# Attention with a fused convolution: maxima across partitions and the output turned by VectorE, the convolution added by GpSimd, high value rows 1088 bytes apart

## What is computed

```
q = Wq x + bq;  k = Wk x + bk;  v = Wv x + bv        # x: 4 images, 256 channels, 64 x 64 pixels; q, k: 32 channels
att = softmax(q^T k / sqrt(32))                       # 4096 x 4096 an image
out = gamma * (v att^T)                               # 256 channels
fused = Wf concat(out, x) + bf                        # 1x1 convolution over 512 channels
```

## Time and profile before

| | us |
|---|---|
| median of 3 runs | 2033.55 (2033.51 to 2033.58) |
| the profiled execution: its time, its span | 2033.3, 2031.4 |
| TensorE busy (share) | 2015.3 (99%) |
| VectorE busy | 1584.9 (78%) |
| ScalarE busy | 1748.9 (86%) |
| GpSimd busy | 1206.1 (59%) |
| TensorE clock granted | 1.00 throughout |
| DMA engines busy, mean | 10% |

### The profile page before, as it was taken

One profiled execution on the slowest core, in us unless ns is written; L12 is line 12 of the kernel. 1 busy time (PEld: TensorE's weight loads), 2 busy tenths in 40 slices (PEclk: granted clock), 3 DMA queues, 4 the chain that ended last, 5 costly groups with the idle time before them and its releaser, 6 DMA issues.

```text
span 2031.4 us, 45017 instructions
## 1 busy us (share of the span) xinstructions
PE 2015.3 (99%) x16232; PEld 1980.4 (97%) x16232; DVE 1584.9 (78%) x2157; ACT 1748.9 (86%) x2373; POOL 1206.1 (59%) x514
## 2 busy tenths in 40 slices
PE   9999999999999999999999999999999999999999
PEld 8999999999899999999989999999998999999999
DVE  6788888886778888888677888888867788888885
ACT  7888888887888888888788888888878888888886
POOL 0467766667056677666605666766660666677665
PEclk9999999999999999999999999999999999999999
DMA  4200000000310000000031000000003100000000
GB/s 136 84 22 22 15 15 21 21 21 12 120 70 22 22 21 15 16 21 21 11 125 65 22 21 21 21 10 21 21 11 130 38 22 21 21 21 18 13 21 17
DMA packets 54081, 69.46 MB, mean 34 GB/s; under 512 B 4048, under 2 KB 37584, under 8 KB 53968
## 3 DMA queue, kind: packets, MB, share of 16 engines
q1 hardware_dynamic: 53696, 67.91, 10.0%
q10 hardware_dynamic: 272, 0.07, 0.0%
HBM read 34.41 MB, written 33.55 MB: 33 GB/s over the span
## 4 chain that ended last, share of the span: by engine, by line
PE 92%; DVE 3%; ACT 3%; issue 2%; DMA 0%; DVEq 0%; ACTq 0%; SPq 0%
PE ps_o L388 72%; PE ps_s L380 11%; PE ps_p L242 3%; PE ps_o L242 2%; PE ps_t L284 1%; ACT queries L478 1%; ACT hi L453 1%; DVE val_lo L676 1%; PE ps_s L259 1%; PE ps_t L276 1%; PE ps_t L269 1%; DVE top L612 1%; DVE lo L599 1%; PE ps_t L242 0%; DVE raw L626 0%
## 5 line engine op out<-in xcount | busy, mean ns | idle before, releaser
L755 POOL TENSOR_TENSOR raw<-raw,top_m 128x1024 f32<-128x1024 f32 x508 | 1205.4, 2413 | 809.1 <-ACT top_m L464 809.1
L631 DVE TENSOR_TENSOR lo<-ps_p,hi 128x1024 fp32r<-128x1024 f32 x512 | 626.9, 1224 | 311.4 <-ACT ps_p L545 311.1
L612 DVE TENSOR_TENSOR top<-ps_s,top 128x512 f32<-128x512 f32 x960 | 660.0, 687 | 55.6 <-ACT raw L459 7.4
L538 ACT ACTIVATE hi<-raw 128x1024 fp32r<-128x1024 f32 x512 | 543.9, 1062 | 145.9 <-PE ps_o L388 141.4
L388 PE MATMUL ps_o<-val_hi,hi 128*128 128x258 f32 x4096 | 664.5, 284 | 4.1 <-ACT hi L538 4.1
L388 PE MATMUL ps_o<-val_lo,hi 128*128 128x256 f32 x4096 | 652.4, 281 | 0.0
L459 ACT ACTIVATE raw<-ps_s 128x512 f32<-128x512 f32 x1024 | 554.1, 595 | 54.7 <-PE ps_s L380 32.0
L388 PE MATMUL ps_o<-val_hi,lo 128*128 128x258 f32 x4096 | 599.3, 284 | 0.0
L388 PEld LDWEIGHTS ps_o<-val_hi,hi 128*128 128x128 f32 x4096 | 562.4, 189 | 5.8 <-issue 4.6
L388 PEld LDWEIGHTS ps_o<-val_lo,hi 128*128 128x128 f32 x4096 | 560.4, 189 | 0.0
L388 PEld LDWEIGHTS ps_o<-val_hi,lo 128*128 128x128 f32 x4096 | 538.7, 190 | 0.0
(11 more groups left out here) (72 smaller groups left out, 1028.3 us busy)
## 6 DMA issues: line engine op xcount, KB each, us to landing
xf<-x SPq DMA_DIRECT2D x32, 512.0 KB, 3.7
conv_d<-conv_st SPq DMA_DIRECT2D x64, 256.0 KB, 2.0
result<-conv_d SPq DMA_DIRECT2D x64, 256.0 KB, 2.6
out<-result SPq DMA_DIRECT2D x64, 256.0 KB, 2.2
raw<-wf2T SPq DMA_DIRECT2D x1, 256.0 KB, 3.9
raw<-wv SPq DMA_DIRECT2D x1, 256.0 KB, 4.3
raw<-wf1T SPq DMA_DIRECT2D x1, 256.0 KB, 4.7
raw<-wkqT ACTq DMA_DIRECT2D x1, 64.0 KB, 2.0
```

Source lines behind the costliest of these rows:

```text
L538: nc.scalar.activation(hi[:, t % 2], raw[:, slot].rearrange("p j i -> p (j i)"), ACT.Exp, scale=SCALE).then_inc(hi_done, 1)
L612: nc.vector.tensor_tensor(top[:, new], scores, top[:, new if half else old], ALU.max).then_inc(max_done, 1)
L631: nc.vector.tensor_tensor(lo[:, t % 2], ps_p[:].rearrange("p h n -> p (h n)"), hi[:, t % 2].bitcast(F32), ALU.subtract).then_inc(lo_done, 1)
L755: nc.gpsimd.tensor_tensor(raw[:, slot], raw[:, slot], top_m[:, r].unsqueeze(1).broadcast_to((P, JQ, I)), ALU.subtract).then_inc(sub_done, 1)
```

## The change

- The turns of the maxima and of the output leave TensorE. `nc.vector.transpose` turns each 32 x 32 square by itself. The maxima: VectorE turns `top_j`, reduces over 32 (leaving eight numbers in each of 128 partitions), brings the four partition groups together with four small copies and two small maxima (`top_across`), and spreads them with another turn (`spread_top`, now in quad 6). ScalarE's copy is gone.
- As the squares are turned in place, the score products read the queries in another order (`turned`), and the output lies in 32-partition groups, so each load of the convolution and each store is four DMAs of 32 partitions with runs of 64 pixels.
- The convolution is added by GpSimd, in its own quad 4, between subtractions; at an image's end in the first chunk of the next projection.
- In the last chunk of a projection the chain of the maxima and `subtract_first` stand on VectorE before the low parts of the values; GpSimd starts after `subtract_first`, and the convolution's first half goes to `ps_t`.
- `val_hi` has rows of 272 numbers (1088 bytes) where it had 258 (1032); 258 are used as before.

```diff
-        val_hi = sb("val_hi", [P, JT, CV], F32R)
+        val_hi = sb("val_hi", [P, JT, C_IN + 16], F32R)
         val_lo = sb("val_lo", [P, JT, C_IN], F32R)
         raw = sb("raw", [P, SLOTS, JQ, I], F32)
         hi = sb("hi", [P, 2, JQ * I], F32R)
         lo = sb("lo", [P, 2, JQ * I], F32R)
         xf = sb("xf", [P, 2, KT, W], F32)
         conv_st = sb("conv_st", [P, KT, W], F32)
-        result = sb("result", [P, OUTS, KT, I], F32)
+        result = sb("result", [P, OUTS, CT, IT * SQ], F32)
+        o_turn = sb("o_turn", [P, CT, IT, SQ], F32)
         o_norm = sb("o_norm", [P, IT, C_IN], F32)
         top = sb("top", [P, 2, 2, I], F32)
         top_m = sb("top_m", [P, OUTS, I], F32)
         top_j = sb("top_j", [P, I], F32)
-        top_col = sb("top_col", [P, IT], F32)
+        top_turned = sb("top_turned", [P, I], F32)
+        top_group = sb("top_group", [P, I // 32], F32)
+        top_over = sb("top_over", [P // 2, I // 32], F32)
+        top_half = sb("top_half", [P // 2, I // 32], F32)
+        top_all = sb("top_all", [P, I // 32], F32)
...
             def load_conv(b, n):
-                sp.wait_ge(stored[n % OUTS], b * (16 * USES[n % OUTS]) + 16 * (n // OUTS + 1))
-                sp.dma_start(result[:, n % OUTS], conv_v[bass.ds(b, 1), :, :, n * I:(n + 1) * I].rearrange(
-                    "b p k n -> p (b k) n")).then_inc(conv_loaded[n % OUTS], 16)
+                sp.wait_ge(stored[n % OUTS], b * (LANDED * USES[n % OUTS]) + LANDED * (n // OUTS + 1))
+                for g in range(GROUPS):
+                    sp.dma_start(result[g * SQ:(g + 1) * SQ, n % OUTS], conv_q[
+                        bass.ds(b, 1), :, :, n * I + g * RUN:n * I + (g + 1) * RUN].rearrange(
+                        "b q c n -> q (b c) n")).then_inc(conv_loaded[n % OUTS], 16)
             def store(b, n):
                 sp.wait_ge(finished, b * BLOCKS + (n + 1))
-                sp.dma_start(out_v[bass.ds(b, 1), :, :, n * I:(n + 1) * I].rearrange("b p k n -> p (b k) n"),
-                             result[:, n % OUTS]).then_inc(stored[n % OUTS], 16)
+                for g in range(GROUPS):
+                    sp.dma_start(out_v[bass.ds(b, 1), :, :, n * I + g * RUN:n * I + (g + 1) * RUN].rearrange(
+                        "b q c n -> q (b c) n"), result[g * SQ:(g + 1) * SQ, n % OUTS]).then_inc(stored[n % OUTS], 16)
...
+            def turned(queries_of):
+                return queries_of.rearrange("r (g i q) -> r i g q", g=GROUPS, i=IT)
...
-                        last = nc.tensor.matmul(ps_s[:, (bank + half) % BANKS, jl], keys[:, j * P:(j + 1) * P],
-                                                queries[:, bass.ds(n * I, I)], start=True, stop=True)
+                        last = nc.tensor.matmul(ps_s[:, (bank + half) % BANKS, jl].rearrange(
+                            "p (i g q) -> p i g q", i=IT, g=GROUPS), keys[:, j * P:(j + 1) * P],
+                            turned(queries[:, bass.ds(n * I, I)]), start=True, stop=True)
...
-            def turn_top(B, done):
-                if done is not None:
-                    pe.wait_ge(finished, done)
-                pe.wait_ge(top_j_done, B + 1)
-                for i in range(IT):
-                    last = nc.tensor.transpose(ps_t[:, i * P:(i + 1) * P], top_j[:, i * P:(i + 1) * P], ident[:])
-                last.then_inc(top_t_ready, 1)
-            def spread_top(B):
-                pe.wait_ge(top_col_done, B + 1)
-                for i in range(IT):
-                    last = nc.tensor.transpose(ps_t[:, I + i * P:I + (i + 1) * P], top_col[:, i:i + 1].broadcast_to((P, P)), ident[:])
-                last.then_inc(m_ready, 1)
-            def turn_out(B):
-                pe.wait_ge(o_scaled, B * IT)
-                for i in range(IT):
-                    for k in range(KT):
-                        last = nc.tensor.transpose(ps_t[:, k * I + i * P:k * I + (i + 1) * P],
-                                                   o_norm[:, i, k * P:(k + 1) * P], ident[:])
-                last.then_inc(o_turned, 1)
...
-                    turn_top(b * BLOCKS, None)
-                    pe.wait_ge(q_out, C + 1)
-                    convolve(ps_p[:, 0], 0, lambda: spread_top(b * BLOCKS))
+                    pe.wait_ge(conv_done, C * 2 - 1)
+                    convolve(ps_t[:], 0)
+                    pe.wait_ge(max_done, b * HALVES + 2 * len(MADE))
                     convolve(ps_s[:, LAST_CONV].rearrange("p j i -> p (j i)"), 1)
...
-                        if t == 1 and not first:
-                            pe.wait_ge(m_done, B + 1)
-                            turn_out(B)
-                        if t == 5 and not last_block:
-                            spread_top(B + 1)
                         scores_ahead(t)
                         pe.wait_ge(lo_done, Q + (t + 1))
                         trail(t, 0)
                         trail(t, 1)
-                        if t == 4 and not last_block:
-                            turn_top(B + 1, None if first else B)
...
+            def turn_top(B):
+                dve.wait_ge(top_j_done, B + 1)
+                nc.vector.transpose(top_turned[:], top_j[:]).then_inc(top_t_done, 1)
             def reduce_turned(B):
-                dve.wait_ge(top_t_ready, B + 1)
-                nc.vector.tensor_reduce(top_col[:].unsqueeze(2), ps_t[:, 0:I].rearrange("p (i j) -> p i j", i=IT), AX_X,
-                                        ALU.max).then_inc(top_col_done, 1)
+                dve.wait_ge(top_t_done, B + 1)
+                nc.vector.tensor_reduce(top_group[:].unsqueeze(2), top_turned[:].rearrange("p (u k) -> p u k", k=32), AX_X,
+                                        ALU.max).then_inc(top_group_done, 1)
+            def top_across(B):
+                dve.wait_ge(top_group_done, B + 1)
+                nc.vector.tensor_copy(top_over[:], top_group[P // 2:P]).then_inc(half_over, 1)
+                dve.wait_ge(half_over, B + 1)
+                nc.vector.tensor_tensor(top_half[:], top_group[0:P // 2], top_over[:], ALU.max).then_inc(half_done, 1)
+                dve.wait_ge(half_done, B + 1)
+                nc.vector.tensor_copy(top_over[0:32], top_half[32:64]).then_inc(quarter_over, 1)
+                dve.wait_ge(quarter_over, B + 1)
+                nc.vector.tensor_tensor(top_all[0:32], top_half[0:32], top_over[0:32], ALU.max).then_inc(quarter_done, 1)
+                dve.wait_ge(quarter_done, B + 1)
+                nc.vector.tensor_copy(top_all[32:64], top_all[0:32]).then_inc(half_filled, 1)
+                dve.wait_ge(half_filled, B + 1)
+                nc.vector.tensor_copy(top_all[64:P], top_all[0:64]).then_inc(top_all_done, 1)
+            def spread_top(B, r):
+                dve.wait_ge(top_all_done, B + 1)
+                nc.vector.transpose(top_m[:, r], top_all[:].unsqueeze(2).broadcast_to((P, I // 32, 32))).then_inc(m_done, 1)
...
-            def add_conv(B, r, loaded):
-                dve.wait_ge(o_turned, B + 1)
-                dve.wait_ge(conv_loaded[r], loaded)
-                nc.vector.tensor_tensor(result[:, r], ps_t[:].rearrange("p (k n) -> p k n", k=KT), result[:, r],
-                                        ALU.add).then_inc(finished, 1)
+            def turn_out(B):
+                dve.wait_ge(o_scaled, (B + 1) * IT)
+                nc.vector.transpose(o_turn[:], o_norm[:].rearrange("p i (c q) -> p c i q", q=SQ)).then_inc(o_turned, 1)
...
                 if last_chunk:
                     early_scores(c)
                     reduce_top(b * HALVES + 2 * MADE[c] + 2)
+                    turn_top(b * BLOCKS)
+                    reduce_turned(b * BLOCKS)
+                    top_across(b * BLOCKS)
+                    spread_top(b * BLOCKS, 0)
+                    subtract_first(b * BLOCKS)
                     values_lo(0)
-                    reduce_turned(b * BLOCKS)
                     values_lo(1)
-                    subtract_first(b * BLOCKS)
                     split_p(b * STEPS, 0)
...
                     if t == 2 and not first:
-                        before = (r + OUTS - 1) % OUTS
-                        use = (n - 1) // OUTS if isinstance(n, int) else (n - 1 - before) // OUTS
-                        add_conv(B - 1, before, b * (16 * USES[before]) + (use * 16 + 16))
+                        turn_out(B - 1)
                     if t == 4 and not last_block:
                         reduce_top(H + 2 * 2 * QUADS)
+                        turn_top(B + 1)
                     if t == 5 and not last_block:
                         reduce_turned(B + 1)
+                        top_across(B + 1)
+                    if t == 6 and not last_block:
+                        spread_top(B + 1, (r + 1) % OUTS)
...
+            def add_conv(B, r, loaded):
+                pool.wait_ge(o_turned, B + 1)
+                pool.wait_ge(conv_loaded[r], loaded)
+                nc.gpsimd.tensor_tensor(result[:, r], o_turn[:].rearrange("p c i q -> p c (i q)"), result[:, r],
```

(49 more changed lines are left out.)

19 lines of the change are left out of this document (6 added, 13 removed).

## The result

The changed kernel takes 2064.94 us (median of 4 runs, 2062.80 to 2066.61) against 2033.57 (4 runs, 2033.51 to 2033.62): ratio 1.0154, 95% interval 1.0141 to 1.0167. The profiled execution has a span of 2061.0 us, 29.6 more than before. It is slower by 31 us; 2050 was predicted, with 2008 to 2085 as range.

The account below looks back on a forecast made before the run. TensorE was taken to bound the kernel. The terms -51.6 - 1.3 - 11.5 + 77.8 + 1.8 + 1.6 = +16.8 us on the profiled execution's 2033.3 gave 2050, range 2008 to 2085.

Parts of the forecast that it names:

- The wait: In quad 0 TensorE waits 1.39 us for a fold, 56 times: +77.8 us.
- The step that decides: From quad 6's start: maxima spread at 2.75 us, ScalarE's exponential at 5.30, fold of quad 7's first half done at 9.14.
- The transposes: Eight transposes a block leave TensorE, saving 0.86 us in each of 60 blocks: -51.6 us, and -1.3 at image starts.
- The rows 1088 bytes apart: High-row value products on TensorE go from 121.0 to about 119.6 ns over 8192 products: -11.5 us.
- the sum: All terms of the forecast added: +16.8 us on the profiled execution's 2033.3.
- Queries in runs, DMAs in fours, adds on GpSimd: Score products' broken reads, up to 33 us, taken as 0; four DMAs and 1.2 us of GpSimd adds a block hidden.
- A sign of being wrong: On TensorE, score products spaced wider than 119 ns would show the forecast wrong.
- Image starts and end: At image starts +0.45 us on TensorE's path, four times, +1.8 us; at the kernel's end +1.6 us.
- Rival (b): Slower: VectorE and GpSimd exclude each other, the chain slips 0.3 to 0.6 us, 2067 to 2084; chance 0.12.
- The margin: GpSimd's batch ends 20.3 us after the maxima, VectorE's next maximum starts 20.3 us after them: nil.
- ring: GpSimd's queue and VectorE's chain behind it, each holding the other from block to block; a 28.1 us block was predicted.
- Rival (a): Faster: TensorE's stall in quad 0 is below 1.09 us, time below 2031; chance 0.20.

Follow-up runs that it names:

- the output's part: Kernel before with only the output turned by VectorE, convolution added by GpSimd, four DMAs, rows 1088 bytes apart; maxima as before, spread in quad 5: 2009.85 us.
- two experiments: High value rows 1032 bytes apart in the changed kernel: 2065.30 us against 2064.94; 1088 in the kernel before: 2033.88 against 2033.85.
- The kernel with one small operation: Changed kernel with one 128x8 copy for the six small operations, leaving out the comparison between the four partition groups: 2009.13 us.
- the maxima's part: Kernel before with only the maxima turned, compared and spread by VectorE, spreading in quad 6; output, add, DMAs and rows as before: 2089.98 us.
- another order in quad 7: Changed kernel where, in quad 7, ScalarE copies scores before its exponentials and VectorE folds their first half before the split: 2073.34 us.

## Why the prediction was right, and where it was not

- **The wait.** The step that decides, the chain from the spreading to the fold, held. In the block with S6 = 1687.11 the maxima come at S6+2.78 (2.75 was predicted), ScalarE starts the exponential at S6+5.30 (5.30), the fold is done at S6+9.13 (9.14), and TensorE's half was due at S6+7.91 (7.88). TensorE started 0.06 us after the fold and not 0.13, a term for which the prediction shows no row, so the half is 1.28 us late and not 1.39. The two score products then take 0.10 us more than usual, which the prediction did not have. Together that is 1.38, as a block grew (28.26 against 26.88); that it meets 1.39 so closely is luck in these two terms, not in the chain. In the block with S6 = 1658.63 the maxima came at S6+3.02, since VectorE's maximum had been held by GpSimd for 0.23 us.
- **The transposes.** 0.43 us for four was right: the output's part alone gives 24 us where 27 - 1.7 = 25 was worked out.
- **The rows 1088 bytes apart: the term that failed.** -11.5 us was predicted; two experiments give 0. The spacing of high-row products stays 120 to 121 ns against 118.7 for low rows in either form; the 1.4 ns beyond the two extra columns are not the rows' starts, and what they are stays open. The rule cited for it (the 16-byte lines of the Trainium skill's "SBUF — State Buffer", section "Door 1: The DMA port swizzle") gives no gain here: by the runs, products of 258 columns do not care whether rows start on a multiple of 16. With this term at 0 the sum is +28.3, and the profiled executions differ by 29.5. It is the largest part of the 15 us between 2050 and the measured median. The medians differ by 31.4; the 2 us more are most likely the clock's, by what the last section shows.
- **Queries in runs, DMAs in fours, adds on GpSimd.** Taken at nothing. DMAs and adds cost nothing by themselves: the output's part has both and gains what its transposes were worth. A sign of being wrong that the prediction named, score products wider apart than 119 ns, did come up (120.6), but it is worth about 2 us, not 33.
- **Image starts and end.** At the first boundary in the profile TensorE waits 1.79 us, now for the low part of the values that stands behind the maxima, and the way from the folds to the first product is 0.1 us longer than before, not 0.45. The end is 1.7 us longer (1.6 was predicted).
- **Rival (b), VectorE and GpSimd holding each other.** The mechanism is real. The rule of the Trainium skill, "SBUF — State Buffer", section "Who interferes with whom", agrees with the trace in that the maximum is held until the subtraction ends (1.72 us in place of 0.425); it ends 0.28 us after that, less than its own 0.425, so not all of it waits. The margin is as thin as said: 28.12 of ring in 28.24 of block. The changed kernel pays little for it, since its 64 maxima take 449 ns in the mean against 425 alone, 1.5 us in all, and the waits are there without GpSimd's adds. The price beyond the margin was mis-sized: not 0.3 to 0.6 us a block but nearly all that is added, 1.19 of 1.25 us in each (the ring's 0.1 us of margin comes off).
- **Rival (a)** needed the maxima before S6+2.45. The kernel with one small operation had them 1 us earlier and came in at 2009, below before, as that threshold says.

## What to carry to other kernels

Work taken from the busiest engine pays only if what now replaces it is ready when it was before: write down the latest start of each handed-over result and follow the queue of every engine that it passes, since everything that stands in order behind the waiting instruction is late too. If a chain is late, start it earlier rather than reorder behind it. When two-input VectorE work and GpSimd share SBUF, place them apart in time with a margin, and look at a duration that varies between equal instructions as the first sign that there is none.

## What the runs showed that I had not expected

- A VectorE maximum over two SBUF tensors (128x256) takes 425 ns alone and 1.72 us in the block shown, where it meets GpSimd's subtraction.
- The chain that ended last names GpSimd for 49%, an engine busy for 62%, and for 47% in the maxima's part, where it has no adds and waits 9.74 us a block. With the maxima as late and another order in quad 7 it names TensorE, for 77%. So the name did not tell what to change. The cure was one VectorE instruction a quad earlier, worth 78 us.
- On VectorE, turning 32x32 squares of float32 goes at the pace of other one-pass operations: 446 ns for 256 and 702 ns for 512 elements a partition.
- The changed kernel's four runs spread over 3.8 us, those of before over 0.1, and the granted clock goes with it: 2062.80, 2064.18, 2065.70 and 2066.61 us had a mean of 0.999, 0.998, 0.997 and 0.997. In the profiled one, the fastest, it is 1.00 from the first products to the last. The trace of the changed kernel with rows of 1032 bytes, an execution of 2064.18 us with blocks of the same length, has a stretch of 3.4 us at 0.50, the lower of its two levels (1.2 GHz), right after TensorE had waited at an image start (TensorE's timeline, then the stretch as a stage):

```profile
1098.88 0.74 PE L389 MATMUL ps_o<-val_hi,hi 128*128 128x258 f32 x4 [1.81 <-DVE val_lo L684]
```

```profile
1099.50:1102.90 3.40, 3.40 (x18) 3.40 (x18) 1.23 (x1) 2.74 (x5) 3.40 (x3) 0.50 0.23 84
```

Half of 3.4 us is lost there, 1.7. That the slower runs of the changed kernel had one to three such stretches is inferred from their mean clocks; they left no trace. Maxima held by GpSimd can't be the spread: they cost 1.5 us in the changed kernel's trace and 1.8 in this one. Why some executions have such a stretch and others not, after the same waits, is open.
